# Indirect reads that go to rows of their own: a bias table stored 128 times, and empty places that read different rows

## The reference

```
# B: one expert per token
max_ind = argmax(softmax(x @ router_w + router_b));  out = 0
for e in range(8):
    a, g = split(x @ w1[e]);  y = silu(a) * g @ w2[e]
    out = where(max_ind == e, y, out)
x = x + tanh(g_ffn[0]) * out * max_prob

# D: experts h and h+1 (mod 8) per token, each with weight 1/2
h = mod(int(x_flat[:, :2].sum(1)), 8);  sel = [h, mod(h + 1, 8)]
for e in range(8):
    w = any(sel == e) / 2
    acc += w * (relu(x_flat @ W1[e] + b1[e]) @ W2[e] + b2[e])
x = x + tanh(g_ffn[1]) * acc
```

## Time and profile before

| | us |
|---|---|
| three runs, median (lowest to highest) | 358.47 (357.48 to 359.72) |
| the profiled execution, its own time | 358.9 |
| its span, first to last instruction | 357.1 |
| TensorE busy, matmul / weight load | 306.1 / 250.3 |
| DVE / ACT / POOL busy | 195.1 / 158.2 / 163.3 |

### The profile page before, as it was taken

One profiled execution on the slowest core, in us unless ns is written; L12 is line 12 of the kernel. 1 busy time (PEld: TensorE's weight loads), 2 busy tenths in 40 slices (PEclk: granted clock), 3 DMA queues, 4 the chain that ended last, 5 costly groups with the idle time before them and its releaser, 6 DMA issues.

```text
span 357.1 us, 8461 instructions
## 1 busy us (share of the span) xinstructions
PE 306.1 (86%) x2870; PEld 250.3 (70%) x2882; DVE 195.1 (55%) x592; ACT 158.2 (44%) x335; POOL 163.3 (46%) x345
## 2 busy tenths in 40 slices
PE   8997995978998999977999999986585996969995
PEld 3657652978998999534677777753265996869895
DVE  7558757233433442465788878656713653435563
ACT  1253602111544552433867676872103663435462
POOL 8550403763665534234555464511470045655542
PEclk9999989896999999999999999999568999989999
DMA  7939992284212210446765552089543012222110
GB/s 209 352 87 372 332 259 74 72 187 111 67 58 67 60 39 31 125 106 171 144 157 148 157 129 60 6 270 289 194 90 16 2 32 59 53 45 53 38 31 25
DMA packets 35889, 42.63 MB, mean 119 GB/s; under 512 B 4868, under 2 KB 30511, under 8 KB 34687
## 3 DMA queue, kind: packets, MB, share of 16 engines
q1 hardware_dynamic: 28872, 31.79, 31.2%
q0 software_dynamic: 3664, 8.73, 10.5%
q10 hardware_dynamic: 3312, 1.58, 1.7%
HBM read 30.84 MB, written 10.96 MB: 117 GB/s over the span
## 4 chain that ended last, share of the span: by engine, by line
PE 60%; DVE 14%; another core or an unknown queue 7%; issue 7%; DMA 4%; ACT 3%; POOL 3%; DVEq 1%; SPq 0%; ACTq 0%; POOLq 0%
PE bank L1254 9%; PE pairB L1045 6%; PE pairA L1045 6%; PE bank L1054 5%; PE bank L1723 4%; PE pairB L1244 4%; PE pairA L1693 3%; PE pairA L1244 3%; PE pairB L1709 3%; PE pairB L344 2%; PE pairA L344 2%; DVE maxi L1793 1%; DMA x<-in_x 1%; PE bank L1741 1%
## 5 line engine op out<-in xcount | busy, mean ns | idle before, releaser
L1254 PE MATMUL bank<-wring,prob 128*128 x312 | 44.3, 287 | 11.8 <-DVE prob L1310 6.9
L1254 PEld LDWEIGHTS bank<-wring,prob 128*128 128x128 f32 x312 | 39.6, 199 | 14.1 <-issue 13.6
L1793 DVE TENSOR_REDUCE maxi<-pairA 128x8 f32<-128x1024 f32 x30 | 36.7, 1222 | 14.3 <-PE pairA L1693 12.9
L1765 ACT ACTIVATE prob<-pairB 128x1024 f32<-128x1024 f32 x30 | 30.7, 1024 | 14.5 <-PE pairB L1709 14.4
L1359 POOL DMA_INDIRECT out_x<-qs,inv_i x16 | 15.9, 996 | 45.5 <-DVE qs L1323 44.4
L1155 POOL DMA_INDIRECT back_d<-ysb,inv_i x23 | 22.7, 988 | 28.1 <-DVE ysb L1116 24.9
L1150 POOL DMA_INDIRECT qs<-rows_b_d,inv_i x23 | 22.4, 976 | 23.3 <-DVE inv_i L760 16.7
L300 POOL TENSOR_TENSOR lnv<-lnv,neg_half 128x4 f32<-128x4 f32 (+1 forms) x12 | 14.8, 1232 | 29.5 <-DVE lnv L295 29.5
L1122 DVE COPY xtT<-bank 128x128 f32<-128x128 f32 x23 | 6.7, 292 | 38.0 <-PE bank L1031 27.0
L1281 ACT ACTIVATE xn<-wring 128x516 f32 x37 | 23.4, 633 | 7.9 <-DVE job_i L850 7.4
L1323 DVE SCALAR_TENSOR_TENSOR qs<-bank,job,qs 128x128 f32 x39 | 13.6, 349 | 23.8 <-PE bank L1254 13.5
(11 more groups left out here) (327 smaller groups left out, 703.5 us busy)
## 6 DMA issues: line engine op xcount, KB each, us to landing
wring<-in_wts SPq DMA_DIRECT2D x8, 768.0 KB, 8.3
wring<-in_wts SPq DMA_DIRECT2D x8, 514.0 KB, 5.2
ks<-kparts_d SPq DMA_DIRECT2D x12, 192.0 KB
qs<-qparts_d SPq DMA_DIRECT2D x12, 192.0 KB
kparts_d<-parts SPq DMA_DIRECT2D x8, 192.0 KB, 2.6
qparts_d<-parts SPq DMA_DIRECT2D x8, 192.0 KB, 3.0
ctx_s<-kparts_d SPq DMA_DIRECT2D x6, 192.0 KB
ctxT<-qparts_d SPq DMA_DIRECT2D x6, 192.0 KB
```

The costliest lines, as they stand in the source:

```text
L1254: j = eng.matmul(bank[1 + i % 2][:, 0:D], act[:, i % 2, c_, :], down_weights(e, o), start=(c_ == 0), stop=(c_ == C1 - 1))
L1765: eng.activation(prob[:, at.half(5), :, :].rearrange("p h t -> p (h t)"), turned_in(at.unit(5))[:, :, :].rearrange("p a t -> p (a t)"), AC ...
L1793: eng.reduce_max(maxi[:, at.half(0), :], scores_in(at.unit(0))[:, :, :].rearrange("p a (h t) -> p (a h) t", t=T), AX).then_inc(s("mx"), 1)
```

## The change

- The table has 8 x 128 rows: row e * 128 + p is expert e's row, for partition p. It is stored by one DMA of 512 KB whose source repeats the eight rows 128 times; SP issues it at the end of `early_keys` instead of POOL in phase A. `b2_i` becomes e * 128 + p, and POOL waits for the table before its first bias gather.
- DVE makes a third set of row numbers, `inv_i[:, 2]`: a filled place keeps its row, an empty place p reads row p. Gathers of phase B from tile 6 on use it; tiles 0 to 5 keep the old one.

```
-        b2pair_d = scratch("b2pair_d", (NE, D))
+        b2pair_d = scratch("b2pair_d", (NE * T, D))
...
-        inv_i = sb("inv_i", [128, 2, KP], i32)
+        inv_i = sb("inv_i", [128, 3, KP], i32)
...
             eng.tensor_scalar(b2a[:, :], b2a[:, :], half_gate[0:NE, :], None, ALU.mult).then_inc(s("b2pair"), 1)
-            eng.wait_ge(s("b2pair"), 3)
-            eng.dma_start(b2pair_d, b2a[:, :]).then_inc(s("b2pair_d"), 16)
...
-            eng.wait_ge(s("b2pair_d"), 16)
...
                 c.link(eng.tensor_scalar(inv[:, 1, :], inv[:, 0, :], -1.0, 1.0, ALU.mult, ALU.add))
+                eng.scalar_tensor_tensor(inv_i[:, 2, :], inv[:, 1, :], part[:, :], inv[:, 3, :], ALU.mult, ALU.add)
...
-                eng.tensor_copy(b2_i[:, :], seg[:, :]).then_inc(s("b2_i"), 1)
+                eng.tensor_scalar(b2_i[:, :], seg[:, :], float(T), part[:, :], ALU.mult, ALU.add).then_inc(s("b2_i"), 1)
...
-                                       in_offset=bass.IndirectOffsetOnAxis(ap=inv_i[:, 0, t.k:t.k + 1], axis=0)).then_inc(xt_in[t.x], 16)
+                                       in_offset=bass.IndirectOffsetOnAxis(ap=inv_i[:, 0 if t.k < AHEAD else 2, t.k:t.k + 1], axis=0)).then_inc(xt_in[t.x], 16)
...
                 eng.wait_ge(s("b2_i"), 1)
+                eng.wait_ge(s("b2pair_d"), 16)
...
             for pair in range(3):
                 load_keys(eng, pair)
+            eng.wait_ge(s("b2pair"), 3)
+            eng.dma_start(b2pair_d.rearrange("(e p) d -> e p d", e=NE), bc(b2a[:, :], 1, T)).then_inc(s("b2pair_d"), 16)
```

## The result

The change made the kernel slower by 0.9%: 361.44 us (median of six executions, 360.76 to 363.74) against 359.48 us for the kernel before in the same session (six, 357.48 to 366.12), ratio 1.0087 with a 95% interval of 1.0053 to 1.0122. Two later comparisons gave 1.0042 (1.0008 to 1.0077) and 1.0040 (1.0009 to 1.0072). The prediction was 351.3 us with a range of 344.5 to 359.5. The profiled execution took 363.74 us, its span was 361.9 us.

The account below looks back on a forecast made before the run. TensorE bounds the kernel where it has work, and stands still when its signals come late. Terms -4.9 - 1.7 - 2.5 + 1.9 = -7.2 us from 358.9 give 351.7, less 0.4 for the median: 351.3 us, range 344.5 to 359.5.

Parts of the forecast that it names:

- the phase D part of the sum: Phase D: without slow one-row bias reads, TensorE's late-signal waits shorten; phase D takes 84 to 86 us instead of 93.
- three terms of -4.9, -1.7 and -2.5 us: Phase D: start wait cut from 6.93 to 2.03 us, clock dip behind it gone, two longer middle waits cut.
- the reads are slow but hidden: Phase D rival: POOL's back-to-back issues hold TensorE's news back, whichever rows are read; 358.0 us, chance 0.24.
- The store's term, +1.9 us: Phase B: the table's store adds to a crowded DMA stretch, one more middling delay, +1.9 us, bounds 0 and 5.4.
- Three to five times as much: DMA engines: the same bytes cost three to five times as much engine time when read from one row.
- Phase B's gathers at zero: Phase B from tile 6 on: shorter gathers aren't waited for, as tiles are gathered six ahead; saved 0, bounds 0 and 3.65 us.
- the small edits at zero: New DVE operation, new `b2_i`, POOL's dropped phase A store and its wait for the table: 0 us each.
- the cost of a cheap gather: Phase D: a bias gather from distinct rows takes 3.5 us of engine time instead of 9.5.

Follow-up runs that it names:

- the eight profiles: Eight kernels with the same twelve gather issues in a row at phase D's start, five with own rows, three with one-row reads; phase D averages 90.6 and 91.7 us.
- extra gathers: Kernel before plus eight 128 KB gathers into an unread buffer, one after the scatter of each of tiles 8 to 15; 370.32 us, ratio 1.0365.
- the early store: The change with the table's store at the start of SP's early part, ahead of the keys' loads; 361.75 us, ratio 1.0109 against the kernel before.
- the places alone: Kernel before with only the third set of row numbers for empty places, table and store as before; 356.68 us, ratio 0.9978.
- four experiments: The change without bias gathers (0.9662); kernel before with bias gathers later (0.9793), with bias and tile gathers spread (0.9672), and that spread plus the change (0.9584).

## Why the prediction was wrong

**The step that failed is the phase D part of the sum**: "Without the slow reads I expect a delay like those where only one tile gather and one bias issue coincide", with its three terms of -4.9, -1.7 and -2.5 us. The reads became as fast as predicted, and the delays stayed: 4.7 us late at the start, half clock behind it, 3.58 and 2.87 us in the middle. Phase D is 90.4 us with own rows and 90.6 without, in one session; by the prediction's own measure, from the first up step to the last down step, it is 91.2 us in the kernel after against 92.5, where 84 to 86 were expected. Moving the bias issues apart, with their slow reads, removed a good part of what making them fast had not (82.8 us). Of -9.1 us, none came that stands clear of the spread (1 us in the averages of the eight profiles). The waits of 1.84 and 3.54 us that the sum compared were not cases with one tile gather and one bias issue: they stand in one run of six issues, from 293.08 to 300.45, and 1.87 and 2.84 in another, from 308.43 to 315.78. The longer wait of each pair is the later one. The half clock behind the start is still there in the kernel after (0.66 over the 5 us from 276); it is absent in the four other profiles with own rows, and in the one with extra gathers, which reads one row.

**The rival "the reads are slow but hidden" was right in its mechanism**, with 358.0 us and a chance of 0.24. Two rows that I had named spoke for it and I gave them too little: one-row reads at the end of phase D that cost TensorE nothing (13.00 of 13.00 us), and those of phase B's empty tiles. Against it stood only that the longest waits were where slow reads pile up; but at the same places the issues pile up too. Two things that always come together can't be told apart by the place where they stand. Its price was too low, since it took 1.3 us off for the shorter reads at the start and put the store at 0.8 us: the time came out above the range for the store and for the session (the kernel before took 1.0 us more than in the runs shown).

**The store's term, +1.9 us**, was of the right size: 1.7 us in the averages of phase B, 0.4% in two of the three comparisons of the change. Its mechanism, another late wait, is not shown. The first of the four waits of phase B, from 70.79, had begun before SP issued the store at 73.77, those from 117.05 and 123.58 come long after it, and kernels without the store have such waits too. That the store can hold others up is shown by the early store: a gather behind it took 9.86 us.

**"Three to five times as much"** for the same bytes from one row holds for the table's rows of 512 bytes; for the 1 KB rows of phase B the prediction's own numbers give 1.5 times (10.3 against 7.0 us).

**Phase B's gathers at zero, the small edits at zero, and the cost of a cheap gather (3.5 us of engine time)** held: 0.9978 for the places alone, and 3.3 to 3.6 us measured.

**What I had not thought of** is that the late news itself isn't the kernel's alone. In a session without it no term of phase D exists.

Open: why TensorE's news is late beside POOL's issues, why the first up step's news is not, and what differs between sessions. POOL's issues and the late news are tied by four experiments that changed phase D by 8 to 15 us, and by the end of the delay in eight profiles; what passes between them was not seen in any trace. In all four a gather was moved or left out together with its issue, so no run separates the issue from the transfer, whatever its rows.

## What to carry to other kernels

When a wait stands where two suspects coincide, look in the trace for each suspect alone before pricing either: here slow reads alone cost nothing at two places, and the price belonged to the gathers as such, close behind one another. Before making indirect DMAs faster, make them fewer or spread them: one wait ahead of each gather, against a counter of finished jobs, gave 2 to 3% in the sessions with late news (and nothing in the others), where 16 gathers nearly three times as fast gave nothing. A one-percent verdict holds for a session; measure the kernel before beside it each time, and look at its own time as well.

## What was not expected of the hardware

- The same program took 357 to 360 us in some sessions and 330 to 331 in others: the difference lies in phases B (78.8 against 69.2 us) and D (93.4 against 74.1), where news of TensorE comes up to 5.8 us late in the one and 0.04 us after the work in the other.
- A store of 512 KB from eight partitions moved 46 GB/s by itself, and a gather behind it took 9.86 us instead of 3.
- A matmul of 8 rows with 128 columns of 4-byte numbers took TensorE 0.48 us; two of 2-byte numbers took 0.28 together.
